# Head attention: which engine turns the split tokens, and where the first turns stand

## The reference

```python
x = x + _L0_attn_a_ref(_layernorm(x, axis=-1))   # 16 heads of 16 numbers, q = k = v
x = x + _L0_ffn_ref(_layernorm(x, axis=-1), ...) # two of eight experts
x = x + _L0_attn_b_ref(_layernorm(x, axis=-1), ...)
x = x + _L0_ffn_ref(_layernorm(x, axis=-1), ...)

# _L0_attn_a_ref:
q = k = v = x.reshape(B, S, 16, 16).transpose(0, 2, 1, 3)
w = einsum('bhqd,bhkd->bhqk', q, k) / sqrt(16)
w = softmax(where(causal, w, lowest))
out = einsum('bhqk,bhkd->bhqd', w, v)
```

## Time and profile before

| What | Value |
|---|---|
| Median of 3 runs | 1636.7 us (1635.93 to 1636.73) |
| The profiled execution, its own time | 1637.01 us |
| Its span, first to last instruction | 1635.3 us |
| PE, DVE, ACT, POOL busy | 1587.8, 1074.7, 986.2, 358.2 us |
| Head attention: first and last exponential | 13.70 us to 519.14 us |
| Granted TensorE clock | 0.999 |

### The profile page before, as it was taken

How to read it: one execution, slowest core, us unless ns; L and a number is a source line. 1 busy time by engine, 2 the same in 40 slices (tenths; PEclk the granted TensorE clock), 3 DMA queues, 4 the chain that set the end, 5 groups by cost and what they waited for, 6 DMA issues and landing times.

```text
span 1635.3 us, 30646 instructions
## 1 busy us (share of the span) xinstructions
PE 1587.8 (97%) x11755; PEld 869.9 (53%) x11755; DVE 1074.7 (66%) x2159; ACT 986.2 (60%) x1260; POOL 358.2 (22%) x466
## 2 busy tenths in 40 slices
PE   6999999999999999999999999999999899999998
PEld 2222222222223666666665666666666566666666
DVE  7533454444335976786556689868999897577554
ACT  6999999999998433443335555555445543353332
POOL 3022122022022000011003644456444400011000
PEclk9999999999999999999999999999999999999999
DMA  4013235000030003011110000100001201411100
GB/s 140 17 30 114 75 117 171 20 15 21 20 111 14 14 14 117 14 20 21 20 20 14 1 1 19 22 14 1 1 1 40 84 12 29 124 27 33 33 14 27
DMA packets 96559, 65.52 MB, mean 40 GB/s; under 512 B 55887, under 2 KB 91294, under 8 KB 96414
## 3 DMA queue, kind: packets, MB, share of 16 engines
q1 hardware_dynamic: 96414, 63.55, 14.1%
HBM read 38.88 MB, written 4.19 MB: 26 GB/s over the span
## 4 chain that ended last, share of the span: by engine, by line
PE 72%; ACT 11%; issue 9%; DVE 6%; POOL 1%; DMA 0%; ACTq 0%; DVEq 0%; SPq 0%; POOLq 0%
ACT a_probs L782 10%; PE a_out L539 7%; PE f_ypsum L1049 7%; PE f_ypsum L1051 7%; PE f_ypsum L1050 7%; PE f_h L1049 7%; PE f_h L1050 7%; PE f_h L1051 7%; PE a_scores L918 4%; PE d_outs L1049 3%; PE d_outs L1050 3%; PE d_outs L1051 3%; PE d_banks L1049 2%; PE d_banks L1051 2%; PE d_banks L1050 2%
## 5 line engine op out<-in xcount | busy, mean ns | idle before, releaser
L782 ACT ACTIVATE a_probs<-a_scores 128x1024 f32<-128x1024 f32 x544 | 500.1, 1212 | 5.6 <-PE a_scores L918 5.5
L1421 ACT ACTIVATE f_gelu<-f_h,f_bcol,s_more 128x512 f32<-128x512 f32 x256 | 198.8, 777 | 407.4 <-PE f_h L1051 392.5
L539 PE MATMUL a_out<-a_probs,a_values 128*32 128x512 f32 (+3 forms) x2560 | 293.2, 539 | 6.6 <-ACT a_probs L782 5.5
L1476 DVE TENSOR_SCALAR f_hh<-f_gelu,f_gates_scaled 128x512 f16<-128x512 f32 x256 | 135.2, 528 | 184.3 <-ACT f_gelu L1421 183.5
L1938 ACT ACTIVATE d_score<-d_dist,d_nksq,s_more 128x512 f32<-128x512 f32 x128 | 104.1, 813 | 187.9 <-DVE d_dist L2083 186.1
L1051 PE MATMUL f_ypsum<-f_w,f_hl 128*128 128x256 f16 x768 | 209.3, 273 | 0.0
L1049 PE MATMUL f_ypsum<-f_w,f_hh 128*128 128x256 f16 x768 | 209.3, 273 | 0.0
L1050 PE MATMUL f_ypsum<-f_w,f_hh 128*128 128x256 f16 x768 | 209.3, 273 | 0.0
L1478 DVE SCALAR_TENSOR_TENSOR f_hl<-f_gelu,f_gates_scaled,f_hh 128x512 f16<-128x512 f32 x256 | 193.3, 755 | 9.1
L918 PE MATMUL a_scores<-a_moving,a_fixed 64*128 64x512 f16 (+3 forms) x1280 | 183.2, 353 | 9.9 <-ACT a_probs L782 3.7
L796 POOL TENSOR_SCALAR_AFFINE_SELECT a_probs<-a_probs 128x256 f32<-128x256 f32 (+1 forms) x224 | 97.9, 452 | 419.0 <-ACT a_probs L782 416.3
(11 more groups left out here) (258 smaller groups left out, 2696.1 us busy)
## 6 DMA issues: line engine op xcount, KB each, us to landing
f_raw<-in_L_ffn_W SPq DMA_DIRECT2D x16, 1024.0 KB, 7.6
f_raw<-in_L_ffn_W SPq DMA_DIRECT2D x24, 512.0 KB, 7.5
a_fixed<-a_moving SPq DMA_DIRECT2D x60, 96.0 KB, 2.3
x<-in_L_attn_a_x SPq DMA_DIRECT2D x7, 512.0 KB, 6.5
out<-x SPq DMA_DIRECT2D x7, 512.0 KB, 3.1
f_raw<-in_L_ffn_W SPq DMA_DIRECT2D x12, 256.0 KB, 3.9
a_fixed<-a_moving SPq DMA_DIRECT2D x60, 32.0 KB, 2.0
f_early_raw<-in_L_ffn_W SPq DMA_DIRECT2D x4, 256.0 KB, 3.4
```

What stands on the lines that cost most here:

```text
L539: mm = pe.matmul(spare[32 * j:32 * j + 32, i % 2, skip:skip + w], values[:, G % 2, kt + tile, j, :], probs[:, u % UR, j % 2, col:col + w], ...
L782: act.activation(probs[:, u % UR], scores[:, 2 * (u % SR):2 * (u % SR) + 2, :], ACT.Exp, scale=HD ** -0.5)\
L1421: act.activation(gel[:, n % HR, :], hps[:, n % 2, :], ACT.Gelu, bias=mix.bcol[:, q, FT * e + j:FT * e + j + 1], scale=pr.scales.hidden)\
L1476: dve.tensor_scalar(hh[:, n % HR, :], gel[:, n % HR, :], gate, None, ALU.mult).then_inc(s_hh, 1)
```

## The change

1. `moving` and `fixed` are laid out as tiles x pair x 128 columns; before it was pair x 2048 columns. A product of 512 queries now streams four runs of 128 numbers; the copies of L556 have one run of 1024 numbers for each partition where they had two of 512.
2. Jobs 0 to 3 are still turned by PE. From job 4 on (`TURNED = 4`) SPq waits for the low halves and issues one DMA transpose from `split_m` straight into `moving` (eight blocks of 128x128), ahead of `copy_fixed` of the same job. PE's turns, the tables and DVE's `place` of these 28 jobs are gone. What waited for s_emov or s_tmov of such a job now waits for the landing (s_turned).
3. PE turns job 1 right after the products of step 0 (before it was step 1), and job 3 whole after step 11 (before, half after 11 and half after 12).
4. The low fixed halves of job 1 are made by POOL, ahead of its first diagonal, and not by DVE.
5. DVE places `fixed` of job 1 behind two of three newton rounds; before it stood ahead of all three.

```diff
+        TURNED = 4
+        def turn_bank(job):
+            return scores[:, 2, :] if job == 2 else spare[:, job % 2, :]
+        def turned(engine, job):
+            if job < TURNED:
+                engine.wait_ge(s_emov, job + 1)
+            else:
+                engine.wait_ge(s_turned, 16 * (job - TURNED + 1))
...
+            def turn(job):
+                sp.wait_ge(s_lo, job + 1)
+                sp.dma_start(tiles_of(moving, job).rearrange("p t r n -> p (t r) n"),
+                             split_m[:, job % 2].rearrange("p t h i j e -> p (t h i j e)"), transpose=True).then_inc(s_turned, 16)
...
             for job in range(BY_ENGINES + 1, CHUNKS * NG):
+                if job >= TURNED:
+                    turn(job)
                 copy_fixed(job)
...
             halves(1)
-            low_fixed(1)
             statistics(1, late)
             place(1)
             first_norm.guess(dve, TPC, 2 * TPC)
+            for i in range(2):
+                first_norm.newton(dve, i)
             place_fixed()
-            for i in range(3):
-                first_norm.newton(dve, i)
+            first_norm.newton(dve, 2)
             split(2)
...
+            pool.wait_ge(s_lo_f, 1)
+            pool.wait_ge(s_xn, 2 * TPC)
+            low_fixed(pool, 1)
...
-                if n == 1:
+                if n == 0:
                     turn(1)
...
-                if n in FIRST_TURN_AT:
-                    turn(*FIRST_TURN_AT[n])
+                if n == 11:
+                    turn(3)
...
-                if GS <= n < GS * (NG - 1) and n % GS in TURN_AT:
-                    job, tiles = TURN_AT[n % GS]
-                    turn(CHUNKS * (n // GS + 1) + job, tiles)
```

More of the change, by code:

```diff
@@ L443, in head_attention @@
         weights.place_scratch(ctx)
-        moving, fixed = ([first, sb(f"a_{n}1", [P, GH // 2, S], F16)] for n, first in (("moving", moving), ("fixed", fixed)))
+        moving, fixed = ([first, sb(f"a_{n}1", [P, TILES, GH // 2, P], F16)] for n, first in (("moving", moving), ("fixed", fixed)))
         split_f = sb("a_split_f", [P, 2, TPC, GH, 4, HD], F16)
@@ L546, in copy_fixed @@
             def copy_fixed(job):
[L548 to L550 removed]
+                turned(sp, job)
                 if job >= BY_ENGINES + 2:
@@ L596, in halves @@
             def halves(job):
-                if job >= 2:
+                if 2 <= job < TURNED + 2:
                     dve.wait_ge(s_tmov, job - 1)
+                elif job >= 2:
+                    turned(dve, job - 2)
                 dve.wait_ge(s_xn, TPC * (job + 1))
@@ L709, in _ @@
                     scales.scan(dve, SCAN_AT[i], mix)
-                if more and c == 2:
-                    place(behind + 1)
-                if more and c == 3:
-                    place(behind + 2)
-                    place(behind + 3)
                 if i == GATHER_AT:
@@ L853, in last_group, with turn @@
                     reads[0].append((mix.s_b2w, 1))
-            def turn(job, tiles=range(TPC)):
-                if tiles[0] == 0:
-                    if job == 2:
-                        pe.wait_ge(s_exp, 8)
-                    else:
-                        free(bank_of(job))
-                        reads[bank_of(job)].append((s_emov, job + 1))
-                    pe.wait_ge(s_lo, job + 1)
-                for t in tiles:
+            def turn(job):
+                if job == 2:
+                    pe.wait_ge(s_exp, 8)
+                else:
+                    free(job % 2)
+                    reads[job % 2].append((s_emov, job + 1))
+                pe.wait_ge(s_lo, job + 1)
+                for t in range(TPC):
                     for r in range(GH // 2):
-                        mm = pe.transpose(turned(job).bitcast(F16)[:, (r * TPC + t) * P:(r * TPC + t + 1) * P],
+                        mm = pe.transpose(turn_bank(job).bitcast(F16)[:, (r * TPC + t) * P:(r * TPC + t + 1) * P],
                                           split_m[:, job % 2, t, 2 * r:2 * r + 2].rearrange("p a i j e -> p (a i j e)"), pr.ident16[:])
-                if tiles[-1] == TPC - 1:
-                    mm.then_inc(s_tmov, 1)
+                mm.then_inc(s_tmov, 1)
             def turn_fixed(job):
@@ L899, in _ @@
                 if kt == 0 and kind in ("full", "first"):
-                    pe.wait_ge(s_emov, job + 1)
+                    turned(pe, job)
                 if kind == "first":
@@ L2153, in hybrid_block @@
                 mix.parts = [early[:, i] for i in range(mix.EARLY)]
-                moving, fixed = (pr.sb(layer)(f"a_{n}0", [P, 2, S], F16) for n in ("moving", "fixed"))
+                moving, fixed = (pr.sb(layer)(f"a_{n}0", [P, TILES, 2, P], F16) for n in ("moving", "fixed"))
                 from_heads = head_attention(pr, block, inputs, cols, w, mix, moving, fixed)
```

59 lines of the change are left out of this document (20 added, 39 removed).

## The result

The median went from 1636.65 us (1635.05 to 1638.58, 14 runs) to **1632.97 us** (1632.43 to 1634.83, 14 runs). The ratio is 0.998, with a 95% interval of 0.9973 to 0.9988, which leaves out 1. The forecast was 1634.0 (1632.9 to 1636.0): the time is in the range, 0.07 above its lower end.

A forecast was written before the change was run, and what follows sets the result against it. ACT's exponentials were taken to bound the first stage, so only idle time ahead of their rows could be won: 1.4 + 0.85 + 0.4 = 2.65 us off, median 1634.0 us, range 1632.9 to 1636.0.

The forecast's parts named there:

- Bulk of the change: nothing: Jobs 4 to 31: removed PE transposes and DVE copies, 41 us, are hidden behind ACT's exponentials; 0 us arrives.
- The new layout at 0: Score products streaming four runs of 128 instead of one run cost 0.
- The DMA transposes hidden: From job 4 on, landings of 4 us, at most 8.2, fit within job 4's 9.4 us; cost 0.
- First two gaps, 1.4 us: ACT's idle 0.70 and 1.84 us: job 1's earlier turn gains 1.4 us (1.1 to 1.7), nearly all at the 11th exponential.
- POOL's operation at nothing: POOL making job 1's low fixed halves, about 1.33 us from 13.5 to 14.9 us, costs 0.
- Fourth gap, 0.85 us: ACT's 0.97 us idle before 39 us: turning job 3 whole starts scores 0.85 us sooner (0.75 to 0.97).
- Later gaps, 0.4 us (0.2 to 0.45): The slip at 394 us and 0.18 us in the row of 77 exponentials go, together 0.4 us.
- Everything wins: Rival, chance 0.14: all reachable ACT idle time, including small slips under PE's turns, goes; 3.5 us, 1633.2.
- Sum: First two gaps, fourth gap and later gaps: 1.4 + 0.85 + 0.4 = 2.65 us (2.05 to 3.1).
- From sum to median: Profiled execution 1637.01 becomes 1634.4; the median, 0.3 lower than the profiled one before, becomes 1634.0.
- DVE and POOL collide: Rival, chance 0.10: POOL delays job 1's halves, step 1's scores come late, newton operations stretch; half of 1.4 goes, 1634.9 to 1635.7.
- No transpose was slow: Rival, chance 0.06 with other DMA costs: transposes from `split_m` over 9.4 us delay job 4; at 16 us, 1640.6.

The follow-up runs named there:

- dma_only: Changed kernel with parts 3, 4 and 5 undone, new layout and DMA transposes kept; 1636.32 us, ratio 1.0 to the kernel before.
- late43: Changed kernel with SPq waiting for 43 exponentials before it issues job 4's DMA transpose; 1638.19 us, one run.
- after_again: The changed kernel itself, timed and profiled a second time; 1632.89 us, ratio 0.9979 to the kernel before.
- no_turn1: Changed kernel with PE's turn of job 1 put back behind step 1; 1635.68 us, one run.
- fixed_first: Changed kernel with DVE's copy into `fixed` of job 1 ahead of all newton rounds again; 1633.49 us, one run.
- low_on_dve: Changed kernel with the low fixed halves of job 1 made by DVE again; 1632.54 us, one run.
- fill_mid: Changed kernel with 22 throwaway identity products on PE in its 1.36 us wait near 899 us; 1632.41 us, ratio 0.9975 to the kernel before.
- one_newton: Changed kernel with the copy into `fixed` of job 1 behind one newton round, not two; 1633.68 us, one run.
- both: Changed kernel with `fill_mid`'s filler plus 105, 18 and 7 throwaway products at PE's start; 1631.91 us, ratio 0.997 to the kernel before.
- best: `both` with 98 products in place of 105 and the copy into `fixed` behind one newton round; 1632.16 us, ratio 0.9976 to the kernel before.

## Why the prediction was right, and where it was off

- **Bulk of the change: nothing.** Right. 14 us of PE and 21 of DVE left, and beside the slips, which the prediction counts by themselves (0.59 us, below), none of it arrived: `dma_only` shows this. The new layout at 0 was right too: the 896 score products of 512 columns take 385 ns in the mean, before and after.
- **The DMA transposes hidden.** Right, and the slack too: 3.1 us at the median against the 4 taken; the worst 7.6 within the bound of 8.2. `late43` found some 6.4 us spare behind the landing.
- **First two gaps, 1.4 us.** 1.455 at the 11th exponential, nothing at the 6th, less 0.11 at the third: 1.34. In `after_again` it is 1.64 at the 11th, less 0.19 at the 6th and 0.11 at the third, again 1.33. The mechanism is shown by `no_turn1` and `fixed_first`, which each give back 1.0 to 1.45 us. Two sentences of the step were wrong. The third exponential was to have 0.2 us of margin. It had none and lost 0.11, since the scores behind the eight transposes stood at 15.0 (15.72 less 0.73) and not at 14.9, and at half pace they took longer than the 0.44 us that was read at full pace. And the copy into `fixed` came at 18.0 and not 17.7: three of the newton operations next to POOL took 0.26 to 0.33 us where 0.16 is usual. The first gap then stayed as it was, held by two things at once: the copy ended at 19.40, and PE, whose transposes of `fixed` at half pace had taken 1.01 us, was free for the scores at 19.50.
- **POOL's operation at nothing.** Right, and so is the other side: `low_on_dve` shows that the move brings 0.07 us.
- **Fourth gap, 0.85 us.** It was 0.96, the upper end of 0.75 to 0.97: the scores followed at once (36.89), and PE's own length left 0.12 and not what I had kept.
- **Later gaps, 0.4 us (0.2 to 0.45).** The mis-sized term: 0.59. It is the 0.27 at 394 us, 0.21 in the row of 77 (0.18 was counted) and 0.11 at one exponential (the 87th) in the row of 387, which the prediction read as unbroken: a pace known to three digits, times 386, can't show 0.11 us. Of the 0.45 that it did count it kept 0.4. *Everything wins* named such slips, and they belonged in the forecast.
- **Sum.** 2.65 forecast, 2.89 on the trace, 2.6 between the groups of times (2.8 beside `after_again`).
- **From sum to median.** This step was wrong: "that execution's time 1634.4", 0.3 less for the median, and 0.3 for the runs' own spread. Before's profiled execution was one with the fall near 900 us. 1.7 us hang on it, and of fourteen times nine of before and six of the changed kernel lie in the upper group or above; the three times shown (1635.93 to 1636.73) did not tell of it. The change itself is worth 2.6 to 2.9 us. The median moved by 3.68 because it also changed groups, and the time stayed in the range by 0.07 us. That was luck: the range was not wide for this reason.

Of the rivals, none came as a whole. Small slips went, as *everything wins* had it. Two signs of *DVE and POOL collide* were there, the scores of step 1 late and newton operations stretched, but they cost 0.11 us and not half of the 1.4: the halves of job 2 ended 0.06 us later than forecast. (Half of the 1.4 on top of 1634.0 is 1634.7, below the 1634.9 at which that rival's range begins.) No transpose was slow.

Left open: why PE's clock becomes full at 16.0 us in some executions and at 19.9 in others (16.5 in before's, 18.6 and 18.2 in the changed kernel's two, 16.0 in `fill_mid`, 16.1 in `fixed_first`, 19.9 in `one_newton`; in `one_newton` and the first of the changed kernel the whole start lies 0.7 us late). Whether the moved turn shifts it can't be told from so few profiles. Why the fall near 900 us comes in some executions, and at which share, is open too; only that filling one wait of 1.36 us takes it away is shown. The few times of before near 1638.6 us (one of 14, and three of 19 and one of 14 beside other kernels) were never profiled: a second fall at the start, like that of `dma_only`, would fit them, but this is not shown. A transpose held back by less than `late43` was not tried, and so the point from which job 4 loses time is worked out and not seen.

## What to carry to other kernels

Ask of every removed instruction whose idle time it ends: 35 us of PE and DVE work under a saturated ACT were worth 0.6 us, and moving two turns and one copy by a step was worth 2.3. Where a chain of two engines bounds a start-up, two reorderings may each seem to be worth nearly the whole gain when taken out alone (1.45 and 1.03 us of 1.34 here): take out one at a time with the other in place, look at both gaps, and don't add the two. Before a median is compared with a sum from one trace, see whether the times fall into groups; here a fall of the clock behind a pause of the matmul engine made them, and throwaway products in the pause removed it.

## What was new about the hardware

- A wait of PE of 1.36 us (ahead of eight products of one column each) was followed by half clock in five of the eleven profiled executions that have it unfilled, at 1.7 us of the time. One of 1.95 us at 21.7 us was followed by half clock in `dma_only` (1.47 us), and not in before and `fixed_first`. With twenty-two products of 128 columns, 1.39 us, in the first of these waits there was no fall in three profiled executions, and no time of the upper group in 26 (`fill_mid`, `both`, `best`).
- The view by stretch shows a clock of 1.00 before the clock's first record (at 16.0 to 19.9 us), but PE runs at half pace there: eight transposes in 1.04 us, in 0.61 later.
- A DMA transpose of 128x1024 f16 within SBUF costs 1.3 us to issue and 3.1 to land, hardly more than one of half the size (1.27 and 2.5).
- Operations of DVE take longer beside POOL's. In the first 30 us of the fourteen traces, all 246 newton operations on DVE that no POOL operation overlaps took at most 0.17 us; of the 73 that one does, 48 took more than 0.20, up to 0.62.
